# A two-layer cross-attention kernel: new order of loads, opening and every stage, and the maxima's transfer issued by the sync engine

## The reference

```
layer 0:  q = x Wq;  k, v = text Wk, text Wv           (60 text tokens)
          p = softmax(q k^T / sqrt(8));  text_out = p v
          k_ip, v_ip from the last 4 tokens
          sem = l2norm(p text) . l2norm(ip)            (per head, row, ip token)
          p_ip = softmax(q k_ip^T / sqrt(8) + 0.5 sem) * side
          x = (text_out + p_ip v_ip) W_out + b_out + x
layer 1:  the same softmax attention over all 64 tokens with its own weights
          (its separate ip branch has 4 more tokens of the same context
          beyond the text length, none here)
          x = attention(x) Wo^T + bo + x
```

## Time and profile before

| | us |
|---|---|
| median of 3 runs (lowest, highest) | 476.2 (472.84, 477.01) |
| the profiled execution's own time | 476.55 |
| its span, first to last instruction | 474.8 |
| TensorE busy | 429.1 (90%) |
| VectorE busy | 301.4 (63%) |
| ScalarE busy | 228.8 (48%) |
| GpSimd busy | 198.0 (42%) |

### The profile page before, as it was taken

How to read it: one execution, slowest core, us unless ns; L and a number is a source line. 1 busy time by engine, 2 the same in 40 slices (tenths; PEclk the granted TensorE clock), 3 DMA queues, 4 the chain that set the end, 5 groups by cost and what they waited for, 6 DMA issues and landing times.

```text
span 474.8 us, 13548 instructions
## 1 busy us (share of the span) xinstructions
PE 429.1 (90%) x5180; PEld 246.8 (52%) x5180; DVE 301.4 (63%) x859; ACT 228.8 (48%) x512; POOL 198.0 (42%) x489
## 2 busy tenths in 40 slices
...
GB/s 211 132 118 183 79 3 87 45 17 96 23 45 86 4 71 59 7 86 43 37 94 4 54 76 4 87 44 53 76 100 53 108 80 50 119 55 213 33 25 43
DMA packets 26284, 33.31 MB, mean 70 GB/s; under 512 B 4553, under 2 KB 17549, under 8 KB 26061
## 3 DMA queue, kind: packets, MB, share of 16 engines
...
...
## 4 chain that ended last, share of the span: by engine, by line
PE 84%; ACT 4%; DVE 3%; DMA 3%; issue 3%; POOL 1%; SPq 0%; DVEq 0%; ACTq 0%; POOLq 0%
PE ps L439 29%; PE ps L583 16%; PE ps L511 9%; PE ps L539 8%; PE ps L617 5%; PE ps L678 3%; PE ps L637 2%; ACT pt L785 2%; PE ps L558 2%; PE ps L662 2%; DMA cst<-in_consts 2%; PE ps L667 2%; PE ps L523 1%; PE ps L633 1%; DMA qs<-mt 1%
## 5 line engine op out<-in xcount | busy, mean ns | idle before, releaser
L785 ACT ACTIVATE pt<-ps 128x512 f32<-128x512 f32 x160 | 93.4, 595 | 40.9 <-PE ps L539 26.6
L889 DVE TENSOR_REDUCE mx<-ps 128x8 f32<-128x480 f32 (+3 forms) x192 | 105.9, 579 | 4.5 <-PE ps L511 4.1
L583 PE MATMUL ps<-pt,gram 64*32 64x256 f32 x1280 | 87.8, 391 | 13.0 <-ACT pt L785 12.7
L558 PE MATMUL ps<-wt,cst 64*32 64x256 f32 x640 | 86.7, 388 | 0.3 <-DVE wt L858 0.3
L589 PE MATMUL ps<-pt,vb 64*32 64x256 f32 x640 | 86.5, 393 | 0.0
L850 DVE TENSOR_TENSOR qr<-ps,qp 80x512 f32<-80x512 f32 x32 | 22.0, 687 | 80.6 <-ACT qp L766 76.5
L439 PE MATMUL ps<-x,wq 80*80 80x512 f32 x128 | 63.9, 623 | 4.0 <-ACT mt L801 1.5
L539 PE MATMUL ps<-qs,ks 101*128 101x256 bf16 x320 | 63.6, 283 | 2.8 <-DMA qs<-mt 2.3
L511 PE MATMUL ps<-ks,qs 96*128 96x128 bf16 x640 | 59.9, 224 | 6.5 <-issue 2.2
L357 POOL TENSOR_TENSOR qp<-qr,qp 80x512 bf16<-80x512 f32 x32 | 37.0, 1157 | 55.0 <-ACT qp L770 55.0
L858 DVE TENSOR_TENSOR wt<-ps,pt 128x512 f32<-128x512 f32 x80 | 54.3, 679 | 8.3 <-PE ps L583 5.4
...
## 6 DMA issues: line engine op xcount, KB each, us to landing
qs<-qp SPq DMA_DIRECT2D x96, 160.0 KB, 4.6
...
out_T<-x SPq DMA_DIRECT2D x16, 160.0 KB, 5.0
...
wk<-in_WK SPq DMA_DIRECT2D x2, 160.0 KB, 5.5
```

Source lines behind the costliest of these rows:

```text
L558: last = nc.tensor.matmul(region(pair, hh), cst[keys_of(hh), C_QSEL + sub * VW_COLS:C_QSEL + (sub + 1) * VW_COLS], wt[keys_of(hh), g % 2, ...
L583: last = nc.tensor.matmul(ps[T * hh + 32 * m:T * hh + 32 * m + 32, bank, sub * S:(sub + 1) * S], gram[keys_of(hh), r, 32 * m:32 * m + 32], ...
L785: nc.scalar.activation(pt[:, g % 2, 2 * c:2 * c + 2, :].rearrange("p a b -> p (a b)"), ps[:, 2 + (g + c) % 2, :], ACT.Exp, scale=SCALE).th ...
L889: nc.vector.tensor_reduce(mx[:, tile, p0:p0 + np_, :], o[:, :, :, 0:nt], AX_X, ALU.max).then_inc(red_done, 1)
```

## The change

It is one change of order and placement with one transfer moved, and no arithmetic is dropped.

- All position tables are new, and MOVED gives single (stage, group, pass) entries a position of their own. `sequence` takes the engine's name. BANK_MOVED gives two entries a bank of their own.
- `mtd` goes from ACT's list to SP's. SP's list in layer 0 reads mtd 6, kd 8, qd 9, mtd 7, and so on; kd 16 and qd 17 now stand behind mtd 15; in layer 1 it reads kd 20, mtd 18, qd 21, mtd 19, and so on; the output stores stand behind mtd 31.
- Loads: the first two batches of x and wq are issued before wkip and have one semaphore, so `q` 0 no longer waits for the constants; the second half of the context is issued when the first has landed; the rest of x comes in seven transfers (`xd`), wk of layer 1 earlier, and the late weights in two parts (`late0` behind mtd 1, `late1` behind qd 7).
- Opening: TensorE's order is key projections, half the ip keys, `q` 0, `q` 1, `setup`, `keys1` in two halves with waits of their own, `sc` of pass 0, `mt` 0, `q` 2. DVE takes the key and query splits of passes 0 to 3 from POOL. `vk` of pass 0 gets bank 4.
- A step of layer 0, TensorE. Before: mt, zt, q, y, vk, st.0, sc.0, st.1, vw, rd.0, sc.1, rd.1, st.2, sc.2, sc.3, st.3, rd.2, sc.4, ot.0, st.4, rd.3, ot.1, rd.4. After: mt, rd.4 of the pass before, zt, q, y, vk, st.0, sc.0, st.1, vw, rd.0, sc.1, st.2, sc.2, rd.1, sc.3, st.3, sc.4, rd.2, st.4, ot.0, rd.3, ot.1. Banks: ot.0 from 0 to 1 and ot.1 from 1 to 0, mt from 0 to 1.
- The same, ACT. Before: exp.3, stat.0, stat.1, exp.4. After: exp.3, stat.0, exp.4, stat.1. DVE. Before: vprep, ipm, red.0, wz, ipr, w.0, red.1, w.1, red.2, red.3, w.2, red.4, on.0, neg, w.3. After: vprep, red.0, wz, ipm, w.0, red.1, red.2, w.1, red.3, red.4, ipr, w.2, neg, on.0, w.3.
- A step of layer 1 begins mt, ot.0, ot.1, y, pv.1, sc.0, sc.1, sc.2, st.0; `q` stands ahead of mt.
- The last pass is cut: its zt, y, ysb and store come in two halves of 128 rows.

The core of the diff:

```diff
-    ("st", 0): (-0.152, 0.087), ("st", 1): (-0.087, 0.13), ("rd", 0): (-0.043, None), ("st", 2): (0.174, 0.217),
-    ("rd", 1): (0.174, None), ("st", 3): (0.304, 0.326), ("rd", 2): (0.37, None), ("st", 4): (0.543, 0.413),
-    ("rd", 3): (0.565, None), ("rd", 4): (0.609, None), ("q4", 0): (0.891, None), ("ot", 0): (1.522, 1.391),
+    ("mt", 0): (-0.4828, -0.3448), ("vk", 0): (-0.2414, 0.2069), ("st", 0): (-0.2069, 0.1724),
+    ("st", 1): (-0.1724, 0.1897), ("rd", 0): (-0.1207, None), ("st", 2): (-0.0862, 0.2414),
+    ("rd", 1): (-0.0517, None), ("st", 3): (-0.0172, 0.2759), ("rd", 2): (0.4138, None),
+    ("st", 4): (0.431, 0.3103), ("rd", 3): (0.4828, None), ("rd", 4): (0.5345, None), ("q4", 0): (0.8621, None),
...
-    ("exp", 2): (0.297, 0.108), ("exp", 3): (0.351, 0.216), ("exp", 4): (0.486, 0.703),
-    ("otev1", 0): (0.784, 0.865), ("otev2", 0): (1.27, 0.973), ("stat", 0): (1.432, None),
-    ("stat", 1): (1.459, None), ("rsq", 0): (1.568, None), ("ipe", 0): (1.946, None), ("ztev", 0): (2.622, 2.189)}
+    ("exp", 2): (0.2292, -0.1458), ("exp", 3): (0.3333, 0.6875), ("exp", 4): (0.3958, 0.75),
+    ("otev1", 0): (0.4583, 0.7917), ("otev2", 0): (1.25, 1.5833), ("stat", 0): (1.375, None),
+    ("stat", 1): (1.4167, None), ("rsq", 0): (1.4792, None), ("ipe", 0): (2.3125, None),
...
-    ("qd", 0): (-2.714, -2.286), ("kd", 0): (-2.571, -3.143), ("late", 0): (-0.857, None),
-    ("outd", 0): (None, 24.571)}
+    ("xd", 0): (-3.8462, None), ("qd", 0): (-2.2308, 9.6154), ("kd", 0): (-1.3077, 9.2308),
+    ("mtd", 0): (0.5385, 11.8462), ("late0", 0): (2.0769, None), ("late1", 0): (5.3077, None),
+    ("outd", 0): (None, 32.3846), ("outd2", 0): (None, 35.4615)}
...
+BANK_MOVED = {("q", 0, 1): 1, ("vk", 0, 0): 4}
+SECOND_HALF, LAST = ("zt2", "ztev2", "y2", "ysb2", "outd2"), N_G - 1
+SPLITS, EARLY = ("kmask", "kr", "kl", "ql"), 4
...
             sp.dma_start(wk[0][:, :, :], WK[0]).then_inc(c_in[0], 16)
+            sp.dma_start(x[:, :, 0:2 * S], xT[:, :, 0:2 * S]).then_inc(x_in[0], 16)
+            sp.dma_start(wq[0][:, :, :], WQ[0]).then_inc(x_in[0], 16)
             sp.dma_start(wkip[:, :, :], WKIP).then_inc(kv_in[0], 16)
-            sp.dma_start(x[:, :, 0:2 * S], xT[:, :, 0:2 * S]).then_inc(x_in[0], 16)
-            sp.dma_start(wq[0][:, :, :], WQ[0]).then_inc(w_in, 16)
             sp.dma_start(cst[:, :], consts).then_inc(w_in, 16)
...
+            def load_x(g, _):
+                sp.dma_start(x[:, :, g * S:(g + 2) * S], xT[:, :, g * S:(g + 2) * S]).then_inc(x_in[g // 2], 16)
...
+            def stack_maxima(g, _):
+                sp.wait_ge(mt_sb, g + 1)
+                slot, b2 = g // 2 % 2, g % 2
+                sp.dma_start(qs[KR:KR + MR, slot, :, b2 * S:(b2 + 1) * S], mt[:, b2, :]).then_inc(m_stacked[b2], 16)
...
-            def keys1(g, _):
-
-                pe.wait_ge(setup_sb, 8)
+            def keys1(g, n):
+
+                pe.wait_ge(setup_sb, 2 + 4 * n)
                 pe.wait_ge(rest_in, 16 * 3)
-                for n in range(2):
-                    project_keys(1, n)
+                project_keys(1, n)
...
+                need(act, c_in[0], 32 * n)
                 act.dma_start(ca[:, :, cols], ctxT[:, :, cols]).then_inc(c_in[n], 16)
...
-            def stack_maxima(g, _):
-                act.wait_ge(mt_sb, g + 1)
-                slot, b2 = g // 2 % 2, g % 2
-                act.dma_start(qs[KR:KR + MR, slot, :, b2 * S:(b2 + 1) * S], mt[:, b2, :]).then_inc(m_stacked[b2], 16)
```

More of the change, by code:

```diff
@@ new lines, with runs @@
+BY_BLOCK = ("kh", "km", "kmask", "kr", "kl", "kd")
+AT = {"PE": PE_AT, "ACT": ACT_AT, "DVE": DVE_AT, "POOL": POOL_AT, "SP": SP_AT}
+BANK_MOVED = {("q", 0, 1): 1, ("vk", 0, 0): 4}
+SECOND_HALF, LAST = ("zt2", "ztev2", "y2", "ysb2", "outd2"), N_G - 1
+ONCE = ("late0", "late1", "setup", "ones", "iplen", "keys1")
+SPLITS, EARLY = ("kmask", "kr", "kl", "ql"), 4
+QUAD_LAG = 3
+LATE = 14
+def runs(engine, what, g):
+    if what in ONCE:
+        return g == 0
+    if what in SECOND_HALF:
+        return g == LAST
+    if what in BY_BLOCK and g % 2 or what == "qd" and g % 2 == 0 or what == "q4" and g != B - 1:
+        return False
+    if what == "xd":
+        return g in range(2, B, 2)
+    if what in SPLITS:
+        return (g < EARLY) == (engine == "DVE")
+    return True
```

235 lines of the change are left out of this document (136 added, 99 removed), and 26 rows, old and new, of tables (DVE_AT, FILL_BANK, MOVED, PE_AT).

## The result

The changed kernel takes **460.7 us** median against 475.1 us for the kernel before, measured beside each other: ratio 0.969, interval 0.962 to 0.976. It is faster, as forecast, but by 14 us and not by 34, and 460.7 lies outside the range of 430 to 456. The profiled execution has a span of 459.9 us, 14.9 less than before. In all that follows medians are of every execution of a version, ratios and intervals leave out executions more than 1.5% above the fastest of their version, and of a_w1, whose profiled execution ran at a granted clock of 0.74 throughout, only times are used.

The account below looks back on a forecast made before the run. TensorE, busy 429.1 of 474.8 us, was taken as the bound, leaving 45.7 idle to win beside clock. Terms 11.3 + 5 + 12.6 - 1.2 + 0.5 + 5.2 + 1.1 = 34.5 gave 440.3, plus 1.75 outside: 442.0, range 430 to 456.

Parts of the forecast that it names:

- rival D: Layer 1: maxima in SP's queue come late behind key and query transfers; 73 us added, 515 in all; chance 0.03.
- the passage into layer 1: Four steps from mt 15: late queries lose 3.3 plus 1.7 of half clock, 3.8 idle goes; net 1.2 us slower.
- a steady step of layer 0: Layer 0's twelve steady steps: the exponential's wait goes, a step falls from 16.0 to 14.9 to 15.0; 12.6 us saved.
- rival A: Layer 0 steps: the vector engine takes the wait's place, step stays at 15.6 or more; 450 us; chance 0.15.
- mt 0 to mt 3: First three steps after the opening: vk 0's bank wait goes and some half clock is regained; 5 us saved.
- I give back a third: From mt 0 to mt 3: of 8.6 us of work lost to half clock, 2.5 is regained as gaps get shorter.
- The opening: Up to mt 0: reordered loads and matmuls bring mt 0 from 41.3 to 30.0; 11.3 us saved.
- rival B: Opening: the first queries are late and gaps bring half clock; 5 to 6 us dearer, 447; chance 0.15.
- The stores: Step from mt 29 to mt 30: stores now follow mtd 31, so it falls from 13.39 to 8.15; 5.2 us saved.
- the tail: End of the kernel, last pass in two halves: 1.1 of its 5.3 us idle saved.
- The move of the transfer itself: Layer 1: maxima issued by SP, mtd 0.4 to 0.8 late behind key transfers; taken at 0, bounds 1 faster, 5 slower.

Follow-up runs that it names:

- a_w1: The changed kernel with the weighting w.1 moved ahead of the reduction red.2 on the vector engine in layer 0: 472.5 us median.
- b_mtdsp: The kernel before with only the maxima's transfer issued by the sync engine, at the place its old positions give: 536.1 us median, ratio 1.129.
- a_late0: The changed kernel with the fourteen late loads issued ahead of mtd 0 instead of behind mtd 1: 465.2 us median, ratio 0.972.
- a_act_st: The changed kernel with the maxima's transfer issued by ScalarE and the first store waiting for the maxima of pass 31: 459.8 us median, ratio 0.966.
- a_mtdact: The changed kernel with the maxima's transfer issued by ScalarE again, right behind its copy: 461.7 us median, ratio 0.971.
- a_act_vk: a_act_st with vk of passes 1 and 2 put in banks 4 and 5: 458.3 us median.
- b_mtdsp2: b_mtdsp with layer 1's query transfers placed ahead of the second maxima of each pair: 474.1 us median, ratio 0.999.
- a_kd16: The changed kernel with kd 16 and qd 17 issued ahead of mtd 15 instead of behind it: 456.3 us median, ratio 0.961.

## Why the prediction was wrong in size, step by step

**The direction** was right, and rival D didn't come: with kd ahead of the first maxima and qd between both, as the new order has them, the cover of 4 us in layer 1 just holds (no wait in ten steps). It was nearer than its chance of 0.03: the same engine with one pair of entries swapped (b_mtdsp) cost 61 us, though by late queries and not by late maxima.

**The step "the passage into layer 1"** failed in two places. The order was read rightly (kd 16 and qd 17 behind mtd 15) and the mechanism named, but the wait was given 3.3 and measured 5.55. The forecast took 4.6 from the last issue to its landing, the median of all query transfers; after, the page says

```profile
qs<-qp SPq DMA_DIRECT2D x96, 160.0 KB, 5.4
```

and the last of six issued back to back took 7.1: that is 2.5 of the miss. It was issued 8.8 after `mt` 15 and not 8.3, 0.5 more, and the cover, estimated at 9.6, was 10.4, 0.8 less: 3.3 + 2.5 + 0.5 - 0.8 = 5.5. With the half clock behind it the queue's order cost 6.8 by experiment, where the forecast had 3.3 + 1.7. And of the 3.8 credited to "ot, zt and y there no longer wait" 1.0 was there: with the queue mended, `mt` 15 to 19 takes 52.3 against 53.3 before. Term: forecast -1.2, measured -5.8.

**The step "a steady step of layer 0"** forecast both chains at 14.9 to 15.0. `mt` to vprep was forecast 6.5, measured 6.39; the hand-over 0.1, measured 0.15. The vector engine's 8.3 "less a wait of 0.41 for POOL" was mis-sized: it is 8.90, or 8.23 without its waits. (8.75 ran to the start of the instruction behind neg, at 170.06; by rows 5 neg ends at 170.15.) The forecast subtracted the one wait of the old order and left out that a new order brings its own: 0.19 and 0.48. That w.0's fell open because ipr, which stood in that place, was moved down the chain, where it still costs its time, is read from the two orders; no run put ipr back. That is rival A (chance 0.15): the vector engine takes the place. It said 15.6 or more, and 15.44 was measured. Three runs show that it is this chain, with waits of 0.67, 0.99 and 1.12 inside it. The forecast's two chains of 14.9 and 15.0 were counted as if they ran apart, and they wait for each other: TensorE up to rd.0, then the vector engine from w.0.

**The step "mt 0 to mt 3"** forecast 5 saved, and 1 was lost. Its bank argument was right for step 0 alone: the same wait stays in step 1 (1.39), and hides a longer one, for the maxima of pass 1, which are issued right behind the query transfers of pass 3 and arrive 0.5 to 0.7 after the last of them. Step 1 was 2.3 longer than before (18.5 and 16.2), step 0 0.7 longer and step 2 2.0 shorter. The clock stayed where it was, at a mean of 0.82 against 0.83, since gaps remained; "I give back a third" had no row for it. Moving vk and then the queries brought 50.2 and 49.3.

**The opening** forecast `mt` 0 at 30.0. Ten profiles of the new opening gave 30.75 to 36.22, five of them between 30.75 and 31.5. The sum by instructions was right to 1.5 us there, the late queries (rival B) are 0.4 to 0.8 in eight of the ten, and what remains is what varies between executions. In a_late0 and a_act_st the keys waited 3.0 and 3.3 for the second half of `ca` and ran at half clock behind it. In the changed kernel (and in a_mtdact and a_act_vk, 33.03 and 32.59) it was the first keys, begun at half clock, here 2.1 longer than at the full clock. So the miss of 3.0 is about 1 of sum and 2 of this execution.

**The stores** were right: 5.2 forecast, 4.6 measured over both steps, 5.1 when done alone. `mt` 28 to 29 is 1.6 shorter as well (7.93), which the forecast didn't have and which is most of the 2.3 saved between `mt` 19 and 29, and the tail gained nothing from its halves (21.0 against 20.8), where 1.1 was forecast.

**The move of the transfer itself**, taken at 0, is near 0 as a sum when its order is right (b_mtdsp2 0.999; a_act_st against a_kd16 from `mt` 0 on, 422.9 and 423.4), with a price and a gain inside. It isn't independent of the rest: it orders the stores for nothing (5.1) and it puts a wait in a queue that others stand in, 6.8 in the passage. The price behind kd, which the forecast bounded at 5 and took at nothing, shows in layer 1: 0 in the changed kernel, but 0.7 to 2.1 in the six other runs with its order there, 4.0 in b_mtdsp2, and 0 in the three runs with the transfer on ScalarE (93.1 each). It is a price of late issue: in a_kd16 the maxima of passes 20, 22 and 26 leave 1.9 to 2.1 after their `mt`, instead of 1.14 to 1.16 in the changed kernel, and each wait ends 2.8 to 2.9 after the issue. The longest such wait anywhere was 1.6, against the 2 a pass weighed in the prediction.

What the prediction drew from the rule that it weighed (the Trainium skill, "DMA: Bandwidth & Descriptors", Queues, rings and completion order), that a transfer of ScalarE's passes a full sync queue, no run here shows. In step 1 the maxima took 6.0 to 6.1 from issue to use when ScalarE issued them (a_mtdact, a_act_st) and 6.2 to 6.4 behind the queries in the sync engine's queue (the changed kernel, a_late0); beside the stores they took 5.6 from ScalarE's queue (rows 6, a_mtdact).
